# A channel-attention kernel on one core: order of shared-half copies and loads, place of the group sums, order of ScalarE's passes

## What is computed

```python
x = x + conv(gn(x))            # gn: group norm, 32 groups of 6 channels, over 6 x 48 x 48 values
# conv, with xt = gn(x) as (image, n = 2304 positions, 192 channels), 8 heads of 24 channels:
q, k, v = split(xt @ w_qkv)    # each (n, 192)
q, k = q / norm over n, k / norm over n, k = k * temperature
attn = softmax(einsum('bhpn,bhnq->bhpq', k, q))     # 24 x 24 for each head: over channels
out = einsum('bhnp,bhpq->bhnq', v, attn) @ w_out + b_out
```

## Time and profile before

| what | value |
|---|---|
| median of 3 runs | 369.4 us (368.01 to 371.26) |
| the profiled execution | 368.91 us |
| its span, from first to last instruction | 367.1 us |
| busy of that span: PE, PEld, DVE, ACT, POOL | 87%, 61%, 78%, 66%, 40% |
| HBM read and written | 29.38 MB, 28.31 MB |

### The profile page before, as it was taken

One profiled execution on the slowest core, in us unless ns is written; L12 is line 12 of the kernel. 1 busy time (PEld: TensorE's weight loads), 2 busy tenths in 40 slices (PEclk: granted clock), 3 DMA queues, 4 the chain that ended last, 5 costly groups with the idle time before them and its releaser, 6 DMA issues.

```text
span 367.1 us, 9393 instructions
## 1 busy us (share of the span) xinstructions
PE 320.4 (87%) x3724; PEld 224.5 (61%) x3724; DVE 285.5 (78%) x703; ACT 240.9 (66%) x432; POOL 145.7 (40%) x129
## 2 busy tenths in 40 slices
PE   0148877999899998999898999999899989999795
PEld 0036655856577566866685666866686658755452
DVE  5899865987799698978789688969788766379674
ACT  1188599648986599748974699649973898620300
POOL 0069579113850188015930288016911386001000
PEclk9999959999999999999999999999999999999899
DMA  7999900015992489527990599328981572027756
GB/s 235 365 297 247 254 11 1 2 46 160 319 301 85 145 269 327 167 87 182 311 320 8 161 302 310 132 88 242 300 278 46 161 254 61 3 86 199 228 172 219
DMA packets 30828, 67.75 MB, mean 185 GB/s; under 512 B 5504, under 2 KB 12096, under 8 KB 30784
## 3 DMA queue, kind: packets, MB, share of 16 engines
q1 hardware_dynamic: 30544, 66.56, 58.0%
q10 hardware_dynamic: 240, 0.59, 0.6%
HBM read 29.38 MB, written 28.31 MB: 157 GB/s over the span
## 4 chain that ended last, share of the span: by engine, by line
PE 36%; DVE 18%; ACT 18%; SPq 8%; issue 6%; POOL 6%; DMA 6%; ACTq 0%; POOLq 0%
PE u_ps L989 16%; PE g_ps L989 10%; ACT h_sb L567 7%; PE s_ps L989 6%; POOL l_sb L495 5%; ACT xn L558 5%; DVE x_sb L914 4%; DMA x_sb<-in_x_dram 4%; ACT tok L605 4%; SPq L386 3%; DVE bnst L782 3%; DVE g_ps L900 2%; DMA wo<-in_L_conv_w_out_dram 2%; SPq L374 2%; DVE tq L898 2%
## 5 line engine op out<-in xcount | busy, mean ns | idle before, releaser
L495 POOL TENSOR_TENSOR l_sb<-xn,h_sb 128x768 f16<-128x768 f32 x63 | 102.8, 1646 | 52.6 <-ACT h_sb L567 52.6
L914 DVE SCALAR_TENSOR_TENSOR x_sb<-u_ps,bias,x_sb 128x384 f32<-128x384 f32 x144 | 85.2, 613 | 18.0 <-PE u_ps L989 16.9
L989 PE MATMUL g_ps<-tok 128*128 128x64 f16 (+1 forms) x864 | 85.9, 239 | 9.5 <-ACT tok L605 8.9
L558 ACT ACTIVATE xn<-x_sb,rb 128x768 f32<-128x768 f32 x61 | 60.2, 1023 | 27.4 <-POOL rb L507 27.4
L989 PEld LDWEIGHTS g_ps<-tok 128*128 128x128 f16 x864 | 56.0, 98 | 35.7 <-ACT tok L605 14.1
L782 DVE BATCH_NORM_STATS2 bnst<-x_sb 128x6 f32<-128x384 f32 x144 | 70.6, 544 | 6.5 <-DMA x_sb<-in_x_dram 6.4
L605 ACT COPY tok<-u_ps 128x384 f32<-128x384 f32 x144 | 64.8, 483 | 15.5 <-PE u_ps L1043 14.5
L989 PE MATMUL u_ps<-h_sb,ml 128*128 128x384 f16 (+1 forms) x336 | 73.1, 328 | 0.0
L567 ACT ACTIVATE h_sb<-x_sb,rb 128x768 f16<-128x768 f32 x63 | 63.3, 1025 | 1.6 <-POOL rb L507 1.6
L1040 PE MATMUL u_ps<-id,h_sb 128*128 128x128 f16 x288 | 48.8, 223 | 6.6 <-DVE l_sb L762 5.8
L501 POOL TENSOR_TENSOR grs<-gvar,minus_half 128x3 f32<-128x3 f32 x8 | 7.1, 882 | 106.8 <-DVE gvar L815 106.8
(11 more groups left out here) (145 smaller groups left out, 532.1 us busy)
## 6 DMA issues: line engine op xcount, KB each, us to landing
x_sb<-in_x_dram SPq DMA_DIRECT2D x48, 384.0 KB, 5.6
out_dram<-x_sb SPq DMA_DIRECT2D x48, 384.0 KB, 3.4
out_dram<-x_sb SPq DMA_DIRECT2D x48, 192.0 KB, 3.1
x_sb<-in_x_dram SPq DMA_DIRECT2D x45, 192.0 KB, 5.1
hl<-h_sb SPq DMA_DIRECT2D x48, 96.0 KB, 3.0
hl<-l_sb SPq DMA_DIRECT2D x48, 96.0 KB, 3.0
x_sb<-in_x_dram ACTq DMA_DIRECT2D x3, 192.0 KB, 4.3
w<-in_L_conv_w_qkv_dram SPq DMA_DIRECT2D x1, 288.0 KB, 7.5
```

The source lines that it names most:

```text
L495: nc.gpsimd.tensor_tensor(l_sb[:, par, t, cols], xn[:, c % XN_RING, :], h_sb[:, par, t, cols], ALU.subtract).then_inc(l_ok, 1)
L558: nc.scalar.activation(xn[:, c % XN_RING, :], xcol(q, t, g * GW, GW), ACT.Identity, bias=rb[:, par, 1, t:t + 1], scale=rb[:, par, 0, t:t + ...
L914: V.scalar_tensor_tensor(out=xs, in0=block_ps(n), scalar=bias[:, t:t + 1], in1=xs, op0=ALU.add, op1=ALU.add).then_inc(out_ok, 1)
L989: return nc.tensor.matmul(dst, lhs, rhs, start=start, stop=stop, skip_group_check=True)
```

## The change

Three edits. (1) SyncE loads in front of the copies of the shared halves: behind k = 2 and 5 the load of k - 2 is issued first, and the copies of the last third are moved from k = 8 to behind k = 10, the last load. (2) The group sums go after block 1 instead of 2, into the bank of block 0 (and so of block 4): DVE's variance follows block 1, and PE's wait for DVE's first step on the sums stands in front of the first product of block 4 instead of between the products of blocks 4 and 5. (3) ScalarE's order: h0 and h1 go in front of the copies of t2, t0, t1 (five passes there instead of three), the copies `p` go behind h3, and the passes behind are x4 h4 x5 h5 x6 x7; in the gram stage h6, h7, x8, h8 follow slots 0, 1, 3, 4 instead of 0, 2, 4, 6.

```diff
-PE_B = {0: ["gram"], 2: ["sums"], "in 4": ["w0"], "in 7": ["w1"], 11: ["scores"], 13: ["squares"]}
-ACT_A = {0: ["h6"], 2: ["h7"], 4: ["x8"], 6: ["exp", "h8"], 11: ["v"], 14: ["m"]}
-ACT_B = ["x0", "x1", "x2", "t2", "t0", "t1", "h0", "h1", "p", "h2", "x3", "x4", "h3", "x5", "h4", "h5", "x6", "x7"]
+PE_B = {0: ["gram"], 1: ["sums"], "in 4": ["w0"], "in 7": ["w1"], 11: ["scores"], 13: ["squares"]}
+ACT_A = {0: ["h6"], 1: ["h7"], 3: ["x8"], 4: ["h8"], 6: ["exp"], 11: ["v"], 14: ["m"]}
+ACT_B = ["x0", "x1", "x2", "h0", "h1", "t2", "t0", "t1", "h2", "x3", "h3", "p", "x4", "h4", "x5", "h5", "x6", "x7"]
...
-VEC_B = {0: ["gram"], 2: ["var"], 3: ["z"], ...
+VEC_B = {0: ["gram"], 1: ["var"], 3: ["z"], ...
...
-                        if k % 3 == 2 and not (isinstance(p, int) and p + 1 == PAIRS):
-
-                            sp.wait_ge(l_ok, halves[g])
-                            copy_parts(1 - par, g)
                     if more and k >= LOAD_LAG:
                         t, g = ROWS[k - LOAD_LAG]
                         sp.wait_ge(stored[t][g], landed[k - LOAD_LAG])
                         load(at, image_in, 1 - par, t, g)
+                    done_group = {2: 0, 5: 1, NC_ + LOAD_LAG - 1: 2}.get(k)
+                    if done_group is not None and p + 1 < PAIRS:
+
+                        sp.wait_ge(l_ok, halves[done_group])
+                        copy_parts(1 - par, done_group)
...
                 elif n in (4, 16):
+                    if sums:
+
+                        pe.wait_ge(gstep, (q + 2) * GVAR + 1)
                     lower_weights(n, True)
                     if n == 4:
                         bank_free(n + 1)
-                        if sums:
-
-                            pe.wait_ge(gstep, (q + 2) * GVAR + 1)
                         lower_weights(n + 1, True)
...
-                        result(p, par, n, norm_next and n == SUMS_AT + 2, lambda: steps_at(f"in {n}"))
+                        result(p, par, n, norm_next and n == SUMS_AT + 3, lambda: steps_at(f"in {n}"))
```

More of the change, by code:

```diff
@@ L69 @@
 PE_A = {0: ["flip"], 8: ["v"], 11: ["m"]}
-PE_B = {0: ["gram"], 2: ["sums"], "in 4": ["w0"], "in 7": ["w1"], 11: ["scores"], 13: ["squares"]}
-ACT_A = {0: ["h6"], 2: ["h7"], 4: ["x8"], 6: ["exp", "h8"], 11: ["v"], 14: ["m"]}
-ACT_B = ["x0", "x1", "x2", "t2", "t0", "t1", "h0", "h1", "p", "h2", "x3", "x4", "h3", "x5", "h4", "h5", "x6", "x7"]
+PE_B = {0: ["gram"], 1: ["sums"], "in 4": ["w0"], "in 7": ["w1"], 11: ["scores"], 13: ["squares"]}
+ACT_A = {0: ["h6"], 1: ["h7"], 3: ["x8"], 4: ["h8"], 6: ["exp"], 11: ["v"], 14: ["m"]}
+ACT_B = ["x0", "x1", "x2", "h0", "h1", "t2", "t0", "t1", "h2", "x3", "h3", "p", "x4", "h4", "x5", "h5", "x6", "x7"]
 POOL_B = ["power", 0, 1, 2, 3, 4, "norms", 5, 6, 7, 8]
 VEC_A = {0: ["soft_in"], 3: ["soft_out"], 7: ["v"], 11: ["m0"], 13: ["m1"], 17: ["stats"]}
-VEC_B = {0: ["gram"], 2: ["var"], 3: ["z"], 5: ["t2"], 7: ["t0", "t1"], 10: ["lo"], 13: ["norms"], 17: ["spread", "bn", "bn", "bn", "bn"]}
+VEC_B = {0: ["gram"], 1: ["var"], 3: ["z"], 5: ["t2"], 7: ["t0", "t1"], 10: ["lo"], 13: ["norms"], 17: ["spread", "bn", "bn", "bn", "bn"]}
 FIRST_PE_A = {17: ["sums"]}
```

## The result

The changed kernel takes 366.79 us (median of 20 runs, 365.22 to 369.3), the kernel before in the same session 370.03 us (20 runs, 366.79 to 372.44). The ratio is 0.9924, with a 95% interval of 0.9897 to 0.9951: faster by 0.8%. The forecast was 366.9 us. Medians and ranges are of all executions; the ratios leave out the few that lie over 1.5% above the fastest of their kernel.

A forecast was written before the change was run, and what follows sets the result against it. PE was taken as the bound, except for waits from late loads and ScalarE's first `tok` copy. 368.91 - 2.3 (loads) + 0.3 (+0.45 - 0.40 in each of six pairs) = 366.9 us; range 364.2 to 370.4.

The forecast's parts named there:

- Part 1: SyncE's queue: loads issued before the shared-half copies end DVE's waits for raw values, gaining 2.3 us (1.1 to 2.34).
- The doubt about load 8: SyncE's queue: load 8 must wait for the last store, so up to 0.7 us may stay in the worst pair.
- Part 2: Result stage: group sums behind block 1 start DVE's variance 0.81 us sooner and remove PE's 0.16 us wait, costing nothing.
- Part 3, t2: Result stage: five passes make t2 0.58 us late, yet the gram stage starts 0.39 us sooner; 0.4 taken per pair.
- the idle time of 0.97 us: Before the first gram product: PE's wait for ScalarE's first `tok` copy, the upper bound of the result stage's gain.
- The wait in front of `squares`: Result stage, PE: `squares` start at 255.30 instead of 254.72, a forecast stall of 1.0 us.
- Part 3, the gram stage: Gram stage: denser passes open gaps of about 0.5 us before slots 2 and 5, costing 0.45 us per pair (0 to 0.58).
- The part that I said comes back at `v`: Gram stage, behind slot 8: some loss returns as DVE no longer idles 1.49 us for POOL's root; 0.45 taken of 0.58.
- Rival A: Gram stage: the two gaps don't show, so six times 0.40 us are gained, 364.2 us in all; chance 0.20.

The follow-up runs named there:

- the fastest version: Changed kernel with gram passes behind slots 0, 2, 4, 6, four passes before t2's copy, `p` before h3: 359.36 us, 0.9724 of the kernel before.
- the kernel without the gaps: Changed kernel with the gram stage's passes back behind slots 0, 2, 4, 6: 362.11 us, ratio 0.9818 against the kernel before.

## Why the prediction was right, point by point

**The stages** came out: result stages 22.36 (22.45 forecast), gram stages 17.53 (17.5), gaps in front of slots 2 and 5, `squares` 0.56 us late (0.58).

**The total** (366.9, measured 366.79) is closer than the working deserves, and a part of that is luck. The forecast took 2.0 us off a profiled execution of 368.91. The stages gave 2.38 us up to the last gram stage. But the kernel before had a median of 370.03 in the session of the comparison, and the drop of the medians is 3.24 us (1.8 to 3.8 by the interval of the ratio). The base was 1.1 us low and the drop 1.2 us small, and the two cancel. What makes the medians differ by more than the stages is not shown; the clock's falls (below) are of that size.

**Part 1** (2.3 us): shown by edit 1 alone, 2.33 us in its profile. One row was matched wrongly: the load issued at 187.94 lands at 194.21, when DVE takes up the chunk behind the one that it had waited 1.61 us for; that wait ended with the load issued just before it, at 187.32, which took 5.7 us. Both were held by the same four copies, so nothing of the sum hangs on it. The sum also treated the gain as the same in any company. Without edit 1 the other two edits run 0.4% over the kernel before, 1.4 us, where I had them at +0.3, which is within the noise; in the fastest version edit 1 is worth 1.8%, which is not. The doubt about load 8 was right in kind: it did not show in the changed kernel's profile, it cost 0.7 us in one pair of the fastest version. Why that landing varies from execution to execution stays open.

**Part 2** (0.16 us and an earlier scale): 22.71 instead of 22.86 in the run with the sums alone, no wait in front of block 4.

**Part 3, t2**: 0.58 us late, and with six, five and four passes `squares` and the stage's end move with t2's copy. That DVE's chain has no reserve is shown, not only read. A term was off by a tenth: the stage gained 0.50, not 0.39 us. I counted the idle time of 0.97 us from the recorded end of PE's last transpose. But where nothing is waited for, the first product starts before that end. The last transpose and the first product, before and in the changed kernel:

```profile
259.76 0.22 PE L1043 MATMUL u_ps<-id,l_sb 128*128 128x128 f16 x1
260.94 0.62 PE L989 MATMUL g_ps<-tok 128*128 128x384 f16 x6 [0.97 <-ACT tok L605]
```

```profile
258.52 0.22 PE L1044 MATMUL u_ps<-id,l_sb 128*128 128x128 f16 x1
258.64 0.61 PE L990 MATMUL g_ps<-tok 128*128 128x384 f16 x6
```

Start to start is 1.18 us before and 0.12 in the changed kernel, so the wait was worth 1.06 us. The run with edit 3 alone is off by the same 0.12. The wait in front of `squares` was forecast as 1.0 us, and that is too much: where they wait for nothing, they start 0.59 us behind the start of the last product (before and in the fastest version), not 0.33; in the changed kernel it is 1.14 (252.35 to 253.49), a loss of 0.55. Their start itself, 17.20 us from the gram stage's end, is where the forecast had it (17.22).

**Part 3, what I missed:** h3 waits 1.12 us for PE's block 11, since its chunk of `h_sb` is still read by the results (the wait is in `split`, L595 of the kernel before). I had ScalarE idle 1 us in front of its first `tok` copy; it idles 0.33 there and 1.12 in front of h3. It cost nothing because that time was spare, and it matters only once t2 is early: then `p` behind h3 costs 0.2 us in each result stage (21.85 against 21.65).

**Part 3, the gram stage** (+0.45): measured +0.45, and +0.67 in the last one, which I had not set apart. The part that I said comes back at `v` does (0.22 us; I had 0.13), but it owes nothing to the denser order: the run with the old gram order has it too, a stage of 16.86. The run without edit 3 has not (17.08), and there DVE still waits 1.49 us for POOL's root, a wait that the new order in the result stage takes away, here as there; so it is that half of edit 3 that brings the 0.22. Against what was at hand the denser order costs 0.67 us in every pair. Rival A (the gaps don't show) fell for this kernel, but the kernel without the gaps was one line away and is 1.1% faster by the ratios.

## What to carry to other kernels

When an engine's list is full behind some wait (here DVE between t2 and the low products), other work may go in front of what ends that wait only as far as it fits before its input is there. ScalarE had 1.01 us to wait for t2 (the runs with the early sums): one more pass fits there. Result stages are 21.65 us with four passes in front, and 22.70 with three (where the order behind t1 differs too). The fifth pass cost 0.5 to 0.7 us for each pair (22.36), the sixth its full 0.92. A net near nothing of several order edits can hide a gain and a loss of the same size, so time each half alone: here one half of edit 3 was worth -0.35 us and the other +0.45 to +0.67 us a pair. And put first in a queue what is needed first, and time it again when the rest has become faster: here that was worth 0.55% at first and 1.8% in the fastest version.

## What of the hardware was not expected

PE's granted clock falls to its lower level (0.50 of full, 1.2 GHz instead of 2.4) for a few us in the last stages of some executions, with the same program there. The PEclk line of the page of the changed kernel, of the kernel before, and of the run with edit 1 alone, 40 slices each:

```profile
PEclk9999969999999999999999999999999999999999
```

```profile
PEclk9999959999999999999999999999999999999899
```

```profile
PEclk9999959999999999999999999999999999999699
```

The length of the same work, from the last gram stage's end to the end of the span, goes with it. Changed kernel, before, and edit 1 alone:

```profile
316.05:363.46 47.41, 39.55 (x356) 24.07 (x354) 33.38 (x66) 6.87 (x18) 1.83 (x2) 0.98 0.55 175
```

```profile
318.43:367.12 48.69, 40.96 (x357) 24.94 (x354) 33.46 (x66) 6.88 (x18) 1.83 (x2) 0.95 0.54 171
```

```profile
315.93:366.30 50.37, 42.62 (x357) 25.55 (x354) 33.51 (x66) 6.88 (x18) 1.83 (x2) 0.93 0.53 165
```

47.4 us without a fall (five of the twelve profiles), 48.7 to 49.1 with an 8 in the third slice from the end (four), 50.4 with a 6 there (three). PE is less busy in this stretch than in the others, 39.55 of 47.41 us, and no edit touches it. The five profiles without a fall are all of kernels with the new order in the result stage, but three others of these fell, and the 20 executions of the changed kernel alone have mean clocks from 0.972 (369.06 us) to 0.989 (365.25 us). So it differs between executions of one kernel, and whether the edits matter too is not shown. In front of the first fall in the run with edit 1 alone PE had been nearly idle: from 336 it was busy 0.23 of 2.00 us, and in the next 2.00 us the mean granted clock was 0.57. But the changed kernel has the same gap (0.35 of 2.00 us from 336) and kept its full clock.

So the clock can account for 1.28 us of the 3.66 between the two profiled executions, and a single execution can't show a change of under about 3 us here. What lets the clock fall in one execution and not in the next was not tried. (All twelve profiles have a low clock in the seventh slice as well, five also in the eighth; that lies ahead of the stages compared here.)
